# Attention stage of a gated decoder layer: four score banks, two banks for turned probabilities, turns four units behind scores, and no clearing instruction ahead of each mask

## The reference, cut to what matters

```python
scores = jnp.einsum('bhnd,bhld->bhnl', q, k) * inv_sqrt_d + mask[:, None]
attn = jax.nn.softmax(scores, axis=-1)
o = jnp.einsum('bhnl,bhld->bhnd', attn, v)
```

## Time and profile before

| what | value |
|---|---|
| time, median of 3 runs | 1017.13 us (1016.01 to 1017.29) |
| time of the profiled execution | 1016.46 us |
| its span, first to last instruction | 1014.7 us |
| mean granted TensorE clock | 0.969 |
| busy: PE, DVE, ACT | 89%, 66%, 57% of the span |

### The profile page before, as it was taken

How to read it: one execution, slowest core, us unless ns; L and a number is a source line. 1 busy time by engine, 2 the same in 40 slices (tenths; PEclk the granted TensorE clock), 3 DMA queues, 4 the chain that set the end, 5 groups by cost and what they waited for, 6 DMA issues and landing times.

```text
span 1014.7 us, 15824 instructions
## 1 busy us (share of the span) xinstructions
PE 899.2 (89%) x5592; PEld 587.9 (58%) x5592; DVE 673.4 (66%) x1870; ACT 573.6 (57%) x1094; POOL 86.9 (9%) x105
## 2 busy tenths in 40 slices
PE   3989998999999787899999999999999899999467
PEld 2868765676767453666444666445666444666233
DVE  5895860524250073798777898777798776799564
ACT  4545233355553132788347788357788447789153
POOL 2000213021120005100100000100000100000100
PEclk9999999999999999799999999999999999999769
DMA  6444556452450059510199110198110188100001
GB/s 195 141 142 159 196 205 228 146 164 86 135 198 1 23 164 197 115 43 2 42 182 191 43 43 2 42 180 186 51 43 1 43 175 196 46 2 1 1 1 42
DMA packets 52270, 102.82 MB, mean 101 GB/s; under 512 B 8924, under 2 KB 8924, under 8 KB 50656
## 3 DMA queue, kind: packets, MB, share of 16 engines
q1 hardware_dynamic: 39872, 71.88, 27.1%
q10 hardware_dynamic: 8160, 17.31, 5.1%
q0 software_dynamic: 4160, 12.62, 4.0%
HBM read 55.62 MB, written 14.75 MB: 69 GB/s over the span
## 4 chain that ended last, share of the span: by engine, by line
PE 36%; DVE 9%; issue 6%; ACT 5%; SPq 4%; DMA 3%; POOL 1%; POOLq 0%; DVEq 0%; ACTq 0%
PE psum L1494 7%; PE psum L1462 6%; PE psum L1567 5%; PE psum L1511 5%; PE psum L1537 5%; SPq L1185 4%; ACT probs L1322 3%; DMA k<-k_lo 3%; PE psum L1429 1%; PE psum L1553 1%; PE psum L1520 1%; DVE amax L1670 1%; DVE xn L1842 1%; DVE stats L1837 1%; DVE xn L1658 1%
## 5 line engine op out<-in xcount | busy, mean ns | idle before, releaser
L1322 ACT ACTIVATE probs<-psum,neg_max 128x512 f32<-128x512 f32 x256 | 175.0, 692 | 46.5 <-DVE neg_max L1732 46.5
L1732 DVE CUSTOM_DVE_ANT_0 psum<-psum,m_in 128x512 f32<-128x512 f32 x256 | 174.0, 703 | 18.3 <-issue 18.3
L1494 PE MATMUL psum<-ident,probs 128*128 128x128 f32 x1024 | 154.2, 275 | 0.0
L1494 PEld LDWEIGHTS psum<-ident,probs 128*128 128x128 f32 x1024 | 127.8, 141 | 19.8 <-issue 2.6
L1462 PE MATMUL psum<-k,q 128*128 128x512 f32 x256 | 125.7, 496 | 15.3 <-ACT probs L1322 6.8
L674 PE MATMUL psum<-w_sb,hT 128*128 128x512 f32 x256 | 117.6, 604 | 5.6 <-ACT hT L566 5.6
L1762 DVE COPY probsT<-psum 128x512 f32<-128x512 f32 x128 | 87.8, 686 | 2.7 <-PE psum L1494 2.5
L1313 ACT COPY probsT<-psum 128x512 f32<-128x512 f32 x128 | 75.3, 588 | 20.3 <-PE psum L1494 20.3
L594 PE MATMUL psum<-xselT_hi,w_hi 128*128 128x256 f32 x256 | 81.8, 320 | 1.6 <-ACT xselT_hi L501 1.6
L674 PEld LDWEIGHTS psum<-w_sb,hT 128*128 128x128 f32 x256 | 47.0, 192 | 55.3 <-issue 48.5
L1462 PEld LDWEIGHTS psum<-k,q 128*128 128x128 f32 x256 | 49.1, 192 | 51.7 <-ACT probs L1322 31.5
(11 more groups left out here) (221 smaller groups left out, 1566.7 us busy)
## 6 DMA issues: line engine op xcount, KB each, us to landing
bw_raw<-in_L_ffn_W_dram ACTq DMA_DIRECT2D x16, 1024.0 KB, 5.3
c_in<-in_ctx_dram SPq DMA_DIRECT2D x8, 1024.0 KB, 5.5
k<-k_hi SPq DMA_DIRECT2D x24, 256.0 KB, 5.9
k<-k_lo SPq DMA_DIRECT2D x24, 256.0 KB, 6.7
q<-q_hi SPq DMA_DIRECT2D x48, 128.0 KB, 3.9
q<-q_lo SPq DMA_DIRECT2D x48, 128.0 KB, 3.4
xres<-in_x_dram SPq DMA_DIRECT2D x4, 1024.0 KB, 5.9
w_raw<-in_L_ffn_w_dram POOLq DMA_DIRECT2D x4, 1024.0 KB, 5.4
```

The costliest lines, as they stand in the source:

```text
L1322: act.activation(probs[:, u % 4, :], psum[u % SCORE_BANKS][:, :], ACT.Exp, scale=-1.0, bias=neg_max[:, u:u + 1], accum_out=prob_sum[:, nt, ...
L1494: mm = pe.transpose(turn_bank(u)[:, l * P:(l + 1) * P], probs[:, u % 4, l * P:(l + 1) * P], ident[:, :])
L1732: dve.tensor_tensor_reduce(bank[:, :], bank[:, :], m_in[:, nt, :], -1.0, LOWEST, ALU.add, ALU.min, neg_max[:, u:u + 1]).then_inc(masked_re ...
```

## The change

The constants change so that scores have four banks (0 to 3) and turned probabilities two (4 and 5). Turns follow scores by four units, so each round holds the same turn as before, and a score one unit later; one more score and one more mask are issued ahead of the loop. The fourth context bank becomes bank 3. VectorE's zero write L1730 and the wait on `probs_ready` ahead of it go away; the mask now carries the wait for the score itself.

```diff
--- before.py
+++ after.py
@@ -1118,9 +1118,9 @@
         x_done = sem("x_done")
         out_stored = sem("out_stored")
 
-        LAG = 3
+        LAG = 4
         RESIDUAL_STEP = 24
-        SCORE_BANKS, TURN_BANKS = 3, 3
+        SCORE_BANKS, TURN_BANKS = 4, 2
         HALF = 2 * P
         HG = 2 * GROUPS
         UH = UNITS // HG
@@ -1129,7 +1129,7 @@
 
         STEPS = UNITS + LAG + UH + 3
 
-        CONTEXT_BANKS = (0, 1, 2, 4)
+        CONTEXT_BANKS = (0, 1, 2, 3)
 
         def turn_bank(u):
             return psum[SCORE_BANKS + u % TURN_BANKS]
@@ -1725,9 +1725,6 @@
 
                     hg, r, nt = unit(u)
                     dve.wait_ge(score_psum, b * UNITS + u + 1)
-                    if u >= 4:
-                        dve.wait_ge(probs_ready, b * UNITS + u - 3)
-                    dve.memset(held[:, u % 4:u % 4 + 1], 0.0)
                     bank = psum[u % SCORE_BANKS]
                     dve.tensor_tensor_reduce(bank[:, :], bank[:, :], m_in[:, nt, :], -1.0, LOWEST,
                                              ALU.add, ALU.min, neg_max[:, u:u + 1]).then_inc(masked_ready, 1)
```

## The result

The changed kernel takes 1021.36 us (median of 6 runs, 1019.85 to 1021.88) against 1017.21 (1014.87 to 1018.62) of the kernel before in the same session: a ratio of 1.0044, 95% interval 1.0027 to 1.0061. It is slower by 0.4%, and the interval lies clear of 1; the forecast of 1022.0 stands 0.6 above it.

The account below looks back on a forecast made before the run. In attention VectorE sets the pace before the first AV group, then a loop through several engines. Three batch rows at +1.26 us and the first at +1.3 make +5.1: 1021.5, said as 1022, range 1016 to 1027.

Parts of the forecast that it names:

- start: six pairs without zero write, one more score: Ahead of a batch row's first AV group: removed zero writes save 0.36 us, a fourth score costs 0.22.
- first half group: First four rounds behind an AV group in a batch row, with no reciprocal yet: +0.04 us.
- stretch with the residual, with one R1 to R4: Rounds where VectorE also does residual rows, one ordinary four-round half included: new bank waits stretch it, +0.10 us.
- three more R1 to R4: Four rounds from one AV group to the next, three times: longer by 0.17 less 0.02 us each, +0.45.
- the last one and the end: Batch row's last four-round half and three closing turns: the last turn waits for ScalarE's copy, +0.81 us.
- The loop goes from the score banks to the turn banks: Four rounds between AV groups: turn waits for VectorE's copy, 4.39 us, replacing the 4.22 us loop through the exponential.
- Rival 2: Two-bank wait never binds, the fourth round's turn starts at 2.36 us: faster, -0.9 per row, 1013.6; chance 0.12.
- rival 3: Slower by more: starved masks start later (+0.05 each), turn starts 0.15 after VectorE's copy; 1028 us; chance 0.08.
- The wait that could have upset the sum: In attention rounds: the exponential now also waits for its own round's turn; taken as met, no size given.
- What follows that turn: Behind the held turn of the fourth round: 0.74 us to the AV group, another 1.00 to the next round.
- Rival 1: VectorE's zero write gives back its whole 59 ns, starved or not: 1017.8 us, no change; chance 0.2.
- R5 to R8 unchanged, 4.51: Four rounds from AVb to the next AVa: ScalarE's chain needs neither third bank, so 4.51 us as now.

Follow-up runs that it names:

- two_turn_banks_only: Kernel before with two turn banks instead of three, three score banks and zero write kept: 1023.58 us, ratio 1.0068 to the kernel before.
- last_turn_own_bank: Changed kernel with the last turn of a batch row in free score bank 0, waiting for no copy: 1017.99 us, ratio 1.0013 to the kernel before.
- no_zero_write: Kernel before without VectorE's zero write and its wait: 1015.72 us, ratio 0.9992 to the kernel before.
- av_later_before: Kernel before with both AV groups and what follows them one round later against the turns: 1006.25 us, ratio 0.9901 to the kernel before.
- score_first_before: Kernel before with the score of the round behind an AV group issued ahead of that group: 1009.05 us, ratio 0.9928 to the kernel before.

## Why the prediction was right, and where its terms were off

| term, per batch row | forecast | measured, second batch row |
|---|---|---|
| start: six pairs without zero write, one more score | -0.36 + 0.22 | +0.16 |
| first half group | +0.04 | 0.00 |
| stretch with the residual, with one R1 to R4 | +0.10 | +0.08 |
| three more R1 to R4 | +0.45 | +0.12 |
| the last one and the end | +0.81 | +0.58 |
| sum | +1.26 | +0.94 (+0.92 end to end) |

- **The loop goes from the score banks to the turn banks: right.** T of R4 starts 2.65 us after S of R1 (611.08 to 613.73; 2.67 in the last half group) where 2.65 was forecast, held by VectorE's copy; S is free. Two small errors cancel in that number: the copy ends 2.53 to 2.55 after S of R1 and not 2.58, and the turn starts 0.12 behind it and not 0.07, which I had read at an AV group behind a copy of ScalarE. two_turn_banks_only shows the same wait with three score banks. Rival 2, faster because that wait never binds, is refuted: it binds in each of these half groups. Of rival 3 the first half is refuted: a starved mask starts 0.54 to 0.55 and ends 1.24 after its score with the zero write and without it. Of the second half, a turn 0.15 behind the copy, 0.12 came. The wait that could have upset the sum did not: in neither kernel does the profile show ScalarE idle ahead of an exponential for anything but a mask.
- **What follows that turn: mis-sized.** I took 0.74 us from turn to AV group "as a turn that is not held needs", counted from the turn's first weight load. In a stream that load starts 0.21 ahead of the turn's first matmul, while the score in front still runs; behind a hold it starts only 0.03 ahead, and AVb comes 0.59 behind it (the last section has the rows). So 0.15 was counted twice. AVa to AVb is 4.28 us, not about 4.40, and the term of +0.15 is +0.04.
- **The end: right in kind, mis-sized in the same way.** The last turn waits for ScalarE's copy, and its own copy starts 0.75 behind the turn's first weight load instead of 0.90. last_turn_own_bank removes 0.57 per batch row: the largest single price of the change.
- **The zero write: mis-sized.** I gave it 0.06 per pair; it is 0.01. Ends of two masks stand 0.65 apart with it and without it. I had read the 0.04 above the spacing behind a copy as the zero write's doing; they are there without it. So the start of a batch row, forecast 0.14 shorter, is 0.16 longer. Rival 1, that all 59 ns come back, falls: no_zero_write gives 0.9992 (0.9979 to 1.0005). The rule of the Trainium skill named there, "VectorE: DVE Perf Modes", section "Rules for kernel authors", asks for fewer operations; for a 128 x 1 write between 128 x 512 operations these runs don't bear it out, and none of them took away a 128 x 512 operation.
- **One more score: right.** Four take 0.87 us in one row of the timeline (560.09), three took 0.64.
- **R5 to R8 unchanged, 4.51: right.** Its cause, AVa's wait for the copy, is shown by av_later_before, which takes the wait away (4.03); score_first_before, which starts the same chain earlier, brings 4.23.
- **The sum.** The attention grew by 3.3 us where 5.1 were forecast: 0.9 for each of three batch rows instead of 1.26, and 0.6 for the first instead of 1.3. Errors of both signs stand in it: the start is 0.30 a row dearer than its terms, the three loops 0.33 and the end 0.23 cheaper, two small terms 0.06. The span grew by 4.9 (1014.7 to 1019.6); 2.1 of that lies between the second and third attention stage (74.85 to 76.98 us). That stretch was in no term. So the closeness of 1022.0 to 1021.36 is partly luck, and the forecast of "slower" is not.

## What to carry to other kernels

In a loop through several engines, count banks stage by stage: from when a bank is filled until its reader lets it go, against the time until it is needed again. Moving a bank from one stage to another moves the loop; it helped nobody here, because the stage that lost it had as little room. When a length read in a busy stream is added behind a wait, count it from the matmul, not from the weight load in front of it. Then ask what the in-order engine holds behind its wait: issuing a consumer one round later (four constants) brought 1.0%, more than any split of the eight banks that was tried. Two edits that each feed the same starving engine may need the same bank, so time them together before adding their gains.

## What the hardware showed that I had not expected

**A clock that falls outside the change.** Between attention stages ScalarE waits for a DMA of `k`, TensorE waits for ScalarE, and TensorE's clock is low for a while around the end of that wait. Windows of the low stretch between the second and third attention stage, before and after:

```profile
685.27:688.70 3.43, 3.43 (x12) 1.33 (x13) 3.24 (x8) 2.39 (x5) 0.00 (x0) 0.57 0.93 191
```

```profile
686.40:693.20 6.80, 5.20 (x16) 1.90 (x17) 4.41 (x9) 3.80 (x6) 0.00 (x0) 0.50 1.07 202
```

The granted clock is 0.50 of 2.4 GHz, the 1.2 GHz level, for 3.4 us before (685.73 to 689.14; the window starts a little earlier, hence its 0.57) and 6.8 us after. What it does to the matmuls there, in the timeline after:

```profile
687.26 2.42 ACT L1335 ACTIVATE hact<-psum,h_unit 128x512 f32<-128x512 f32 x4 [3.70 <-DMA k<-k_lo]
...
688.00 0.19 PE L1527 MATMUL psum<-ident_b 128*128 128x1 bf16 x1 [3.73 <-ACT hact L1335]
...
689.78 1.87 PE L1537 MATMUL psum<-bw1T,qxT 128*128 128x512 fp8e4 x4
...
693.24 1.02 PE L1537 MATMUL psum<-bw1T,qxT 128*128 128x512 fp8e4 x4
```

Four matmuls take 1.87 us at the low level and 1.02 at the high one. Of the 2.1 us, 1.3 are a later start: from the last AV group to the matmul behind the wait 47.71 us pass before (685.27, TensorE idle for 2.47) and 48.97 after (688.00, idle for 3.73). The other 0.9 go with the clock: from that matmul to the next batch row's first score 27.14 us pass before and 28.01 after. The code there is the same in both kernels. The 42 such stretches of the 14 profiles go in steps. From the matmul to the score they take 25.5 us where the clock stays high, 26.9 to 27.1 where it is low for 3.4 us, and 28.0 to 28.4 where it is low for 6.8; the idle time ahead of the matmul is 2.4 to 2.8 us or 3.5 to 3.8. From last AV group to first score that makes 73.2 to 77.4 us. So a time can be some us away from what its attention says, and stages of one kernel differ in this as much as kernels do. What decides which step comes is not settled: no run here moved the DMA alone.

**A turn's row of weight loads starts while the score in front still runs.** T of R4 in the kernel before, not held:

```profile
630.25 0.57 PEld L1494 LDWEIGHTS psum<-ident,probs 128*128 128x128 f32 x4
...
630.46 0.60 PE L1494 MATMUL psum<-ident,probs 128*128 128x128 f32 x4
```

Its four weight loads take 0.57 us and start 0.21 ahead of its first matmul. The held one after (631.32 and 631.35 above) takes 0.42 and starts 0.03 ahead. That looks as if a held turn were cheaper, but from its first matmul to the AV group 0.53 us pass before (630.46 to 630.99) and 0.56 after (631.35 to 631.91). The first matmul itself starts 2.69 us after S of R1 before and 2.70 after. So the row of weight loads shows a wait of 0.40 here, while AVb comes only 0.04 later against S of R1 (3.22 and 3.26): the old loop through the exponential had been nearly as long as the new one.

**An AV group has a fixed price on TensorE,** about 0.34 us beside what its matmuls take (from 0.77 and 1.20), an estimate from two group sizes. Whether it is the switch between 128-column and 32-column weights or something else at the group's ends is not shown.
